# First feed-forward: turn back one step later, with a new order of work on VectorE, ScalarE and TensorE

## The reference, cut to what matters

```
def act_quant(x):
    scale = 127.0 / jnp.clip(jnp.max(jnp.abs(x), axis=-1, keepdims=True), 1e-05)
    return jnp.clip(jnp.round(x * scale), -128, 127) / scale
...
h = bit_linear(x, w1)                                   # 256 -> 1024
h = depthwise_conv1d(h.transpose(0, 2, 1), conv_w, conv_b)
h = h.transpose(0, 2, 1)
h = jax.nn.silu(h)
return bit_linear(h, w2)                                # 1024 -> 256
...
x = x + jnp.tanh(g_ffn[0]) * _L0_ffn_ref(_layernorm(x, axis=-1), ...)
```

## Time and profile before

| | us |
|---|---|
| median of 3 runs | 1910.52 |
| the runs | 1905.21 to 1912.49 |
| the profiled execution | 1910.83 |
| its span | 1909.0 |
| first up of the stage | 193.74 |
| last down of the stage ends | 451.78 |

### The profile page before, as it was taken

How to read it: one execution, slowest core, us unless ns; L and a number is a source line. 1 busy time by engine, 2 the same in 40 slices (tenths; PEclk the granted TensorE clock), 3 DMA queues, 4 the chain that set the end, 5 groups by cost and what they waited for, 6 DMA issues and landing times. The chain is left out here.

```text
span 1909.0 us, 29587 instructions
## 1 busy us (share of the span) xinstructions
PE 1644.5 (86%) x10149; PEld 1246.8 (65%) x10149; DVE 1159.0 (61%) x2579; ACT 882.7 (46%) x1795; POOL 321.8 (17%) x359
## 2 busy tenths in 40 slices
PE   7797788887899898799997399999936999979998
PEld 5454345556677666688884189999925888854446
DVE  4678567676456567889886823222257889841216
ACT  2332577764532221465653355555544566533213
POOL 0000000000000102111100345555561111001110
PEclk9898899998899999999998699999968999979999
DMA  6000000003000000100005822222261000010002
GB/s 200 1 1 1 1 1 1 1 1 127 1 1 1 1 1 1 31 1 1 2 1 195 291 65 73 73 70 73 70 196 28 1 2 1 2 47 1 0 1 89
DMA packets 62849, 78.83 MB, mean 41 GB/s; under 512 B 13179, under 2 KB 52655, under 8 KB 62319
## 3 DMA queue, kind: packets, MB, share of 16 engines
q1 hardware_dynamic: 42967, 47.35, 7.4%
q0 software_dynamic: 7584, 20.72, 3.5%
q10 hardware_dynamic: 12152, 8.85, 1.5%
HBM read 58.16 MB, written 18.74 MB: 40 GB/s over the span
## 5 line engine op out<-in xcount | busy, mean ns | idle before, releaser
L3002 PEld LDWEIGHTS moe_bank<-moe_xt,moe_w1e 128*128 128x128 f32 x1264 | 155.0, 194 | 5.7 <-DVE moe_xt L2850 1.8
L3002 PE MATMUL moe_bank<-moe_xt,moe_w1e 128*128 128x128 f32 x1264 | 155.8, 277 | 1.1 <-DVE moe_xt L2850 1.1
L3012 PE MATMUL moe_bank<-moe_w,moe_xin 128*128 x632 | 149.3, 379 | 0.0
L3076 ACT ACTIVATE moe_xin<-moe_bank,moe_b 128x128 f32<-128x128 f32 x316 | 90.3, 368 | 124.9 <-PE moe_bank L3002 124.9
L372 PE MATMUL l0f_hb<-l0f_xt,f_w 128*128 128x512 f32 x256 | 125.7, 623 | 5.3 <-DVE l0f_a L306 3.8
L1471 POOL TENSOR_TENSOR all_x<-all_x,l1x_fbias 128x256 f32<-128x256 f32 x32 | 23.3, 732 | 589.9 <-DVE l1x_fxn L204 589.9
L3012 PEld LDWEIGHTS moe_bank<-moe_w,moe_xin 128*128 128x128 f32 x632 | 114.0, 190 | 12.3
L209 DVE BATCH_NORM_STATS2 all_stats<-all_x 128x6 f32<-128x256 f32 x256 | 104.0, 421 | 5.2
L2859 DVE TENSOR_TENSOR moe_y<-moe_bank,moe_b2r 128x256 f32<-128x256 f32 x79 | 33.5, 424 | 118.8 <-PE moe_bank L3012 118.8
L2919 POOL DMA_INDIRECT moe_results<-moe_y,moe_row x79 | 78.0, 988 | 125.1 <-DVE moe_y L2859 121.8
L2850 DVE COPY moe_xt<-moe_bank 128x256 f32<-128x256 f32 x79 | 33.5, 424 | 106.6 <-PE moe_bank L2990 106.6
(11 more groups left out here) (484 smaller groups left out, 3804.8 us busy)
## 6 DMA issues: line engine op xcount, KB each, us to landing
moe_w<-in_L_ffn_W SPq DMA_DIRECT2D x32, 512.0 KB, 10.6
moe_w<-moe_results SPq DMA_DIRECT2D x16, 512.0 KB, 8.8
all_x<-in_x SPq DMA_DIRECT2D x4, 1024.0 KB, 13.2
out_x<-all_x SPq DMA_DIRECT2D x8, 512.0 KB, 2.9
f_w<-in_L_ffn_w_T SPq DMA_DIRECT2D x2, 1024.0 KB, 13.5
moe_inputs<-moe_xin ACTq DMA_DIRECT2D x8, 256.0 KB, 7.2
moe_inputs<-moe_w1e ACTq DMA_DIRECT2D x8, 256.0 KB, 7.7
moe_b2r<-in_L_ffn_b SPq DMA_DIRECT2D x1, 2048.0 KB, 14.2
```

The source lines that it names most:

```text
L3002: ins = nc.tensor.matmul(out, w1e[:, at:at + P], xt[:, u, c * P:(c + 1) * P], start=(c == 0), stop=(c == DC - 1))
L3012: ins = nc.tensor.matmul(bank[4 + u][:, 0:D], ht[:, u, c * P:(c + 1) * P], w2[:, ds(e * (HC * D) + c * D, D)], start=(c == 0), stop=(c == ...
L3076: ins = nc.scalar.activation(ht[:, u, m * P:(m + 1) * P], bank[1 + u][:, m * P:(m + 1) * P], ACT.Gelu, bias=b1[:, ds(e * HC + m, 1)])
```

## The change

All three engines get a new order in the loop over g, and zq a second buffer (by t % 2). In one slot VectorE now does largest_hidden(t-1) first, then update(t-3), both taps, dequantise, largest_input, stats(t-3). TensorE does turn_back(t-2, 0), up half 0, turn_back(t-2, 1), up half 1, turn_x, down(t-2) and last turn_z(t). ScalarE does centre(g-1) first, then quantise_x, copy_q(t-2, 0), both quantise(t-1), copy_q(t-2, 1), norm, silu(g-1), copy_x. So a row tile is quantised one slot after it was turned and turned back in the slot after that. The loops run one pass longer. The special place of turn_z for t over 24 is gone.

```diff
--- before.py
+++ after.py
@@ -233,7 +233,7 @@
         xt = s.sb("xt", [P, 2, DC, S])
         a = s.sb("a", [P, 3, S])
         z = s.sb("z", [P, RING, S])
-        zq = s.sb("zq", [P, 2, HM * P])
+        zq = s.sb("zq", [P, 2, 2, HM * P])
         q2 = s.sb("q2", [P, 2, M, P], BF16)
         silu_in = s.sb("silu_in", [P, M])
         hb = [s.ps(f"hb{k}", [P, S]) for k in range(2)]
@@ -325,25 +325,25 @@
                     dve.wait_ge(s.x_ready, t + 1)
                     tile_stats(nc, sh, t).then_inc(s.stats_ready, 1)
 
-                for g in range(END + 3):
+                for g in range(END + 4):
                     t = g - LAG
                     b, m = g // M, g % M
-                    if 0 <= t - 2 < T:
-                        update(t - 2)
+                    if 0 <= t - 1 < T:
+                        largest_hidden(t - 1)
+                    if 0 <= t - 3 < T:
+                        update(t - 3)
                     if 1 <= g <= SLOTS:
                         conv(g - 1, 0)
                         conv(g - 1, 1)
                     if b < B - 1 and m >= HM:
                         dequantise((b + 1) * TB + 2 * (m - HM))
                         dequantise((b + 1) * TB + 2 * (m - HM) + 1)
-                    if 0 <= t < T:
-                        largest_hidden(t)
                     if b < B - 1 and m < HM:
                         largest_input(b + 1, 2 * m, 2)
                         if m == HM - 1:
                             input_scales(b + 1)
-                    if 0 <= t - 2 < T:
-                        stats(t - 2)
+                    if 0 <= t - 3 < T:
+                        stats(t - 3)
                     if g == 2:
                         dve.wait_ge(s.w2_scaled, 1)
                         c.link(nc.vector.tensor_scalar(w2[:, :, :], w2[:, :, :], MAGIC, 1.0, ALU.subtract, ALU.min))
@@ -399,7 +399,7 @@
                     else:
                         pe.wait_ge(s.q2_ready, 2 * (t - 1) + half + 1)
                     for i in range(HM):
-                        ins = nc.tensor.transpose(back_bank(t, half)[:, i * P:(i + 1) * P], zq[:, half, i * P:(i + 1) * P], sh.ident[:, :])
+                        ins = nc.tensor.transpose(back_bank(t, half)[:, i * P:(i + 1) * P], zq[:, t % 2, half, i * P:(i + 1) * P], sh.ident[:, :])
                     ins.then_inc(s.back_ps, 1)
 
                 def down(t):
@@ -417,28 +417,25 @@
                 for t in range(0, TB, 2):
                     turn_x(t, 0)
                 fed = TB
-                for g in range(END + 2):
+                for g in range(END + 3):
                     t = g - LAG
                     b, m = g // M, g % M
-                    if t > TAIL and t < T:
-                        turn_z(t, 0)
-                        turn_z(t, 1)
-                    if 0 <= t - 1 < T:
-                        turn_back(t - 1, 0, fed)
+                    if 0 <= t - 2 < T:
+                        turn_back(t - 2, 0, fed)
                     if g < SLOTS:
                         up(g, 0)
-                    if 0 <= t - 1 < T:
-                        turn_back(t - 1, 1, fed)
-                    if 0 <= t <= TAIL:
-                        turn_z(t, 0)
-                        turn_z(t, 1)
+                    if 0 <= t - 2 < T:
+                        turn_back(t - 2, 1, fed)
                     if g < SLOTS:
                         up(g, 1)
                     if b < B - 1 and m >= HM:
-                        turn_x(fed, max(0, 2 * t))
+                        turn_x(fed, max(0, 2 * (t - 1)))
                         fed += 2
-                    if 0 <= t - 1 < T:
-                        down(t - 1)
+                    if 0 <= t - 2 < T:
+                        down(t - 2)
+                    if 0 <= t < T:
+                        turn_z(t, 0)
+                        turn_z(t, 1)
 
             @block.scalar
             def _(act):
@@ -478,9 +475,9 @@
 
                 def quantise(t, half):
                     act.wait_ge(s.sc2_ready, t + 1)
-                    if t:
-                        act.wait_ge(s.back_ps, 2 * (t - 1) + half + 1)
-                    nc.scalar.activation(zq[:, half, :], z_bank(t)[:, half * HM * P:(half + 1) * HM * P], ACT.Copy, bias=MAGIC,
+                    if t >= 2:
+                        act.wait_ge(s.back_ps, 2 * (t - 2) + half + 1)
+                    nc.scalar.activation(zq[:, t % 2, half, :], z_bank(t)[:, half * HM * P:(half + 1) * HM * P], ACT.Copy, bias=MAGIC,
                                          scale=sc2[:, t:t + 1]).then_inc(s.zq_ready, 1)
 
                 def copy_q(t, half):
@@ -498,25 +495,26 @@
                 nc.scalar.activation(silu_in[:, :], cb[:, :], ACT.Silu).then_inc(s.table_loaded, 1)
                 act.wait_ge(s.table_loaded, 1)
                 nc.scalar.activation(w2[:, :, :], w2[:, :, :], ACT.Copy, bias=MAGIC, scale=wscale[:, 1:2]).then_inc(s.w2_scaled, 1)
-                for g in range(END + 2):
+                for g in range(END + 3):
                     t = g - LAG
                     b, m = g // M, g % M
+                    if 1 <= g <= SLOTS:
+                        centre(g - 1)
                     if b < B - 1 and m >= HM:
                         quantise_x((b + 1) * TB + 2 * (m - HM))
                         quantise_x((b + 1) * TB + 2 * (m - HM) + 1)
-                    if 1 <= g <= SLOTS:
-                        centre(g - 1)
+                    if 0 <= t - 2 < T:
+                        copy_q(t - 2, 0)
                     if 0 <= t - 1 < T:
-                        copy_q(t - 1, 0)
-                        copy_q(t - 1, 1)
+                        quantise(t - 1, 0)
+                        quantise(t - 1, 1)
+                    if 0 <= t - 2 < T:
+                        copy_q(t - 2, 1)
                     if b < B - 1 and m < HM:
                         norm((b + 1) * TB + 2 * m)
                         norm((b + 1) * TB + 2 * m + 1)
                     if 1 <= g <= SLOTS:
                         silu(g - 1)
-                    if 0 <= t < T:
-                        quantise(t, 0)
-                        quantise(t, 1)
                     if b < B - 1 and m >= HM:
                         copy_x((b + 1) * TB + 2 * (m - HM))
```

## The result

| | before | after |
|---|---|---|
| median, us | 1911.57 (6 runs) | 1917.40 (6 runs) |
| profiled execution, us | 1910.83 | 1918.37 |
| its span, us | 1909.0 | 1916.5 |
| stage: first centre tap to the end of the last down, us | 252.8 | 263.3 |
| of it to slot 31's second up half | 210.3 | 190.7 |

The changed kernel takes 1.0034 of the time of before (95% interval 1.002 to 1.0049): 0.3% slower, inside the 0.5% called no change. The forecast was 1912.6, range 1900 to 1922. Behind the small sum stand two large terms. The loop slots gain 19.6 us and the drain loses 30.2, so the stage itself is 10.5 us longer.

What follows compares the result with a forecast made beforehand. The prediction took a chain through ScalarE to bound the loop slots and another the drain. Lead 10.6 + 9.2 = 19.8 us, less 17.7 for the drain, less 4.2 for the clock: 2.1 slower, 1912.6 us, range 1900 to 1922.

Steps and rivals of the forecast that it cites:

- What bounds the loop: Loop slots: a chain through ScalarE bounds them; after, plain slots 6.14 us for 6.55, with input work 7.67 for 8.35.
- Slots 4 to 8: Centre tap ahead of the two quantise_x drops their 0.80 us a slot; lead at slot 8 is 3.7 us.
- Slots 8 to 12: Maximum and quantise work comes a slot later; lead at slot 12's second up half 10.6 us, 3.7 from the slots before.
- The total lead of 19.8: Way to slot 31's second up half: 10.6 us by slot 12 plus 9.2 from slot 12 to 31.
- The drain's chain: After slot 31, down waits for copy_q behind quantise: 5.47 us a pass, drain 60.2 for 42.5, loss 17.7.
- the drain keeps its 3.61: Rival, drain: copy_q isn't down's last wait, so only the extra pass is paid; 1894 us, chance 0.10.
- The clock: TensorE in the drain: five slow stretches at about 0.85 us each cost 4.2 us, bounds 0 and 15.7.
- The sum: Whole kernel: lead 19.8, less drain loss 17.7, less clock 4.2, makes it 2.1 us slower.
- the rival with the slow drain: Slots 32 to 40: turn_z and down at the lower clock throughout, 1.74 us a pass; 1925.8 us, chance 0.10.

Runs made afterwards that it cites:

- p2: Changed kernel with the two quantise_x ahead of the centre tap on ScalarE again: 1921.01 us, ratio to before 1.0052.
- d5: Changed kernel with 16 unused identity transposes per drain pass where TensorE waits for copy_q, left out in slot 32: 1910.09 us, ratio to before 1.0001.
- d1: Changed kernel with copy_q(t-2, 1) ahead of the two quantise(t-1) on ScalarE from slot 32 on: 1892.04 us, ratio to before 0.9898.
- e3: d2 with turn_z(t) between the up halves again in the loop slots, ahead of the second: 1876.56 us, ratio to before 0.9810.
- d2: d1 with turn_z(t) ahead of down(t-2) on TensorE in passes with t over 24: 1884.67 us, ratio to before 0.9858.
- e2: e1 with update(t-3) behind the two dequantise on VectorE in slots with input work: 1884.64 us, ratio to before 0.9867.
- p1: Kernel before with the centre tap ahead of the two quantise_x on ScalarE: 1899.99 us, ratio to before 0.9942.
- p3: Changed kernel with VectorE's largest value behind taps and dequantise, as before the change: 1965.52 us in one execution.
- d3b: Changed kernel with 16 unused identity transposes in every drain pass, slot 32 included, run once more for its time line: 1914.05 us in one execution.
- d4: Changed kernel with turn_z first in the pass on TensorE for t over 24, ScalarE's new order kept: 1908.56 us, ratio to before 0.9978.
- e1: d2 with turn_x behind down(t-2) instead of ahead of it in slots with input work: 1880.31 us, ratio to before 0.9847.

## Why the prediction was right

*What bounds the loop: right.* The chain of the earlier trace rows was the bound, and TensorE's own work took its place. The sum said 6.14 us for plain slots, 6.06 came; 7.67 with input work, 7.70 came. From slot 12's to slot 31's second up half it said 129.5, and 128.6 came (257.96 to 386.60).

*Slots 4 to 8: right.* Lead 3.7 forecast, 3.6 measured (first to eighth centre tap 38.4 for 42.0), and undoing the centre tap's place alone gives it back (p2).

*Slots 8 to 12: right, a little high.* Lead at slot 12 was 10.6 in the prediction and is 9.6 (62.0 us from the first centre tap to slot 12's second up half, for 71.6). The walk holds up to turn_z(1); from there to turn_z(2) it gave 6.15 us, and 7.03 came (247.47 to 254.50). The total lead of 19.8 came out as 19.6.

*The drain's chain: right.* The work before the clock was given as 60.2 us; with the clock held it is 60.4 (d5). That copy_q's place is the cause, d1 shows. The 42.5 it was set against are not quite free of the clock: the window for "1.00 now" starts at 419, and a slow stretch stands at 415.3 to 418.7. The rival "the drain keeps its 3.61" needed ScalarE to be through earlier; it isn't.

*The clock: mechanism right, size wrong.* This is the term that was mis-sized: 4.2 us taken, 12.3 measured. I took slots 5 to 8 as the nearest rows, a third of the time as slow, and 0.85 us for each of five slow stretches. There were nine, at 1.37 us each. The pass grows to 6.84 us, in which one slow stretch of 3.4 us comes again each time, over just the two pieces on the chain, down and turn_z (1.37 longer together, of the 1.74 that was the upper bound). The pass length fell in step with the stretches instead of sliding past them. That is not bound to happen: in p2, whose drain is written the same, the stretches do slide, passes go from 6.73 over 5.49 to 7.05 us, there are seven stretches, and the drain is 3.9 us shorter (68.7).

*The sum.* 19.6 less 17.9 (60.4 for 42.5) less 12.3 is 10.6 us slower for the stage, where I had 2.1. The medians moved by 5.8, which lies inside the range. That the median came within 4.8 us of the forecast, with the stage 8.5 off its sum, is in part luck: in the profiled executions the changed kernel's stage began 3.1 us earlier, with TensorE 30.7 us at the low clock ahead of it for 41.0, over the same instructions. The forecast of no change beyond 0.5% holds, but it is nearer than it looks to the rival with the slow drain, which was given 0.10 and 1925.8: its mechanism, down and turn_z slowed in every pass, is what happened from slot 33 on, at 12.3 us for its 15.7.

## What to carry to other kernels

When a software pipeline is deepened so that an engine's in-order queue no longer waits on itself, write out the same queue for the passes in which the filling work has run out; here one copy standing behind another step's quantise cost 27 us there (the clock's part included), while TensorE had no idle time in the plain loop slots with the same order, and the order may differ between the two. Price each idle gap that such a chain leaves on TensorE twice, once at full clock and once with every piece on the chain at the lower level, and look whether the period can lock to the slow stretches. Try the parts of a reordering alone: centre tap first gave 11 us by itself, 8.8 of them inside the stage.

## What the runs showed of the hardware

- In the changed kernel the slow stretches of 3.4 us fell in step with the loop: from slot 33 on they began 6.8 us apart, one in every pass of 6.84 us, while a pass at full clock takes 5.49 (d5).
- Transposes can hold the clock up. With 16 more of them per pass TensorE's granted clock was 1.00 over the drain, for 0.78. The Trainium skill, TensorE: Matmul & The Clock Gate, Part 4 (PE-mode transpose), says that the full clock doesn't engage for transposes, as they don't count as busy in the same way; d5 measures the opposite for these fp32 transposes.
- The first centre tap, with the same instructions ahead of it, came at 192.8 to 199.2 us in the profiled executions, and the clock goes with it. TensorE spent 27.3 us at granted clock 0.50 ahead of it (from 20 us on) in e3, where it came at 192.8; 30.7 in after, d1, d2, e2, p1 and p3, at 195.4 to 197.2; 41.0 in before, d3b, d4, d5, e1 and p2, at 198.3 to 199.2. It begins early: the same eight matmuls in e3 and d5 (different line numbers, same work), with the clock at 1.00 in e3 and at 0.50 from 26.4 to 33.3 us in d5:

```profile
26.27 3.66 PE L902 MATMUL l0x_sb<-l0x_xt,l0x_queries 128*77 128x512 f32 x8 [0.69 <-ACT l0x_xt L659]
...
27.20 6.65 PE L906 MATMUL l0x_sb<-l0x_xt,l0x_queries 128*77 128x512 f32 x8 [0.69 <-ACT l0x_xt L663]
```

What decides which of the three it is, no run shows. Lengths inside a stage are the safer comparison below 5 us.
